# The first attention's output bias as one fp32r product of full height instead of four one-row fp32 products

## The reference

```python
y = jnp.moveaxis(ys, 0, 1).reshape(b, t, H) @ Wout.T + bout
z = x + y
mu = z.mean(-1, keepdims=True)
var = ((z - mu) ** 2).mean(-1, keepdims=True)
return (z - mu) / jnp.sqrt(var + LN_EPS) * ln_g + ln_b
```

## Time and profile before

| what | us |
|---|---|
| median of 3 runs (1953.53 to 1953.88) | 1953.6 |
| the profiled execution's own time | 1950.02 |
| its span, first to last instruction | 1948.2 |
| PE busy | 1700.6 (87%) |
| DVE busy | 1412.5 (73%) |
| ACT busy | 1026.3 (53%) |
| POOL busy | 572.8 (29%) |
| FFN's first product starts at | 385.40 |

### The profile page before, as it was taken

One profiled execution on the slowest core, in us unless ns is written; L12 is line 12 of the kernel. 1 busy time (PEld: TensorE's weight loads), 2 busy tenths in 40 slices (PEclk: granted clock), 3 DMA queues, 4 the chain that ended last, 5 costly groups with the idle time before them and its releaser, 6 DMA issues.

```text
span 1948.2 us, 26315 instructions
## 1 busy us (share of the span) xinstructions
PE 1700.6 (87%) x7480; PEld 1301.4 (67%) x7480; DVE 1412.5 (73%) x2367; ACT 1026.3 (53%) x1765; POOL 572.8 (29%) x441
## 2 busy tenths in 40 slices
PE   3677676599999999999688898999699999999998
PEld 2344344387787778787366666666487787778787
DVE  6899998667777777777367666665577777777776
ACT  1121111166666666655376766767566666666665
POOL 1455555501101110400167666767501101110100
PEclk8788777599999999999699989989899999999999
DMA  2000001100000000100000000000100000000001
GB/s 77 0 1 0 0 0 33 50 1 16 16 1 16 16 0 0 33 1 1 0 1 1 1 1 0 0 1 1 33 1 17 17 0 17 16 0 0 0 1 43
DMA packets 23716, 20.14 MB, mean 10 GB/s; under 512 B 1626, under 2 KB 19166, under 8 KB 23646
## 3 DMA queue, kind: packets, MB, share of 16 engines
q1 hardware_dynamic: 23646, 19.29, 3.3%
HBM read 17.18 MB, written 2.10 MB: 10 GB/s over the span
## 4 chain that ended last, share of the span: by engine, by line
PE 69%; DVE 10%; issue 9%; POOL 7%; ACT 3%; DMA 0%; SPq 0%; DVEq 0%; POOLq 0%; ACTq 0%
PE pair L347 12%; PE pair L349 12%; PE pair L348 12%; PE bank L347 7%; PE bank L348 6%; PE bank L349 6%; POOL ARENA_R L735 3%; DVE XN L390 2%; DVE ARENA_R L1348 2%; PE pair L1168 2%; POOL ARENA L646 1%; DVE ARENA L457 1%; PE pair L1097 1%; PE pair L1098 1%; DVE ARENA L1486 1%
## 5 line engine op out<-in xcount | busy, mean ns | idle before, releaser
L1344 DVE TENSOR_TENSOR ARENA<-ARENA,pair 128x512 f32<-128x512 f32 x512 | 351.5, 687 | 289.9 <-PE pair L349 212.8
L772 ACT ACTIVATE ARENA<-bank 128x512 f32<-128x512 f32 x512 | 304.2, 596 | 347.2 <-PE bank L349 345.8
L347 PE MATMUL pair<-ARENA_R 128*128 128x512 f32 (+1 forms) x1080 | 427.2, 396 | 32.4 <-DVE ARENA_R L1348 17.9
L348 PE MATMUL pair<-ARENA_R 128*128 128x512 f32 (+1 forms) x1080 | 421.9, 391 | 0.0
L349 PE MATMUL pair<-ARENA_R 128*128 128x512 f32 (+1 forms) x1080 | 421.9, 391 | 0.0
L1348 DVE TENSOR_TENSOR ARENA_R<-ARENA,ARENA_R 128x512 fp32r<-128x512 f32 x512 | 375.6, 735 | 11.9
L766 ACT ACTIVATE ARENA_R<-ARENA 128x512 fp32r<-128x512 f32 x512 | 321.2, 627 | 64.5 <-DVE ARENA L1344 64.0
L735 POOL TENSOR_TENSOR ARENA_R<-ARENA,ARENA_R 128x512 fp32r<-128x512 f32 x192 | 250.3, 1317 | 120.2 <-ACT ARENA L909 115.5
L347 PEld LDWEIGHTS pair<-ARENA_R 128*128 128x128 f32 x1080 | 203.8, 189 | 86.3 <-DVE ARENA_R L1348 23.0
L589 POOL CAST ARENA_R<-ARENA 128x1536 fp32r<-128x1536 f32 x12 | 23.2, 1937 | 756.4 <-PE pair L349 756.4
L349 PEld LDWEIGHTS pair<-ARENA_R 128*128 128x128 f32 x1080 | 203.6, 189 | 42.8
(11 more groups left out here) (207 smaller groups left out, 2463.8 us busy)
## 6 DMA issues: line engine op xcount, KB each, us to landing
ARENA<-in_L_ffn_Wg_dram SPq DMA_DIRECT2D x16, 256.0 KB, 2.7
ARENA<-in_L_ffn_Wu_dram SPq DMA_DIRECT2D x16, 256.0 KB, 3.1
ARENA<-in_L_ffn_Wd_dram SPq DMA_DIRECT2D x16, 256.0 KB, 3.6
X<-in_L_attn_a_x_dram SPq DMA_DIRECT2D x8, 256.0 KB, 6.5
out_dram<-X SPq DMA_DIRECT2D x8, 256.0 KB, 2.3
CST<-in_tables_dram SPq DMA_DIRECT2D x1, 832.5 KB, 4.7
ARENA<-in_tables_dram SPq DMA_DIRECT2D x1, 768.0 KB, 4.3
CST<-in_tables_dram SPq DMA_DIRECT2D x1, 259.0 KB, 4.9
```

Source lines behind the costliest of these rows:

```text
L347: pe.matmul(dst, wh, xh, start=start, stop=False)
L348: pe.matmul(dst, wh, xl, start=False, stop=False)
L772: act.activation(SG[:, k % 2, :], bank[k % 2], ACT.Silu).then_inc(s.sil, 1)
L1344: v.tensor_tensor(HF[:, k, :], SG[:, k % 2, :], bank[2 + k % 2], ALU.mult).then_inc(s.mul, 1)
```

## The change

The bias becomes a matrix of 128 rows, BBA, whose row 0 is the fp32r rounding of `bout`, row 1 the rest that the rounding left, and all others zero. One fp32r product of ONESR (all ones, 128x128) with BBA, repeated four times by a zero stride to 512 columns, writes the whole bank with the bias; the four products with WOUT then add to it.

```diff
                     pe.wait_ge(A.y, old.n + 1)
+                    pe.matmul(by_sub(bank[4]), ONESR[:, :], spread(BBA[:, :], SUB), start=True, stop=False,
+                              skip_group_check=True)
                     for k in range(SUB):
                         cols = slice(k * P, (k + 1) * P)
-                        pe.matmul(bank[4][:, cols], Y[:, old.p, cols], WOUT[:, :], start=True, stop=False)
-                        x = pe.matmul(bank[4][:, cols], ONES[0:1, :], BROW[:, 0:C], start=False, stop=True)
+                        x = pe.matmul(bank[4][:, cols], Y[:, old.p, cols], WOUT[:, :], start=False, stop=True,
+                                      skip_group_check=True)
                     x.then_inc(A.z, 1)
```

```diff
@@ SP
-            sp.dma_start(BROW[:, 0:C], row(a_bout)).then_inc(ld.ba, 16)
+            sp.wait_ge(pr.ones, 3)
+            sp.dma_start(BA0[0:2, :], row(a_bout).broadcast_to([2, C])).then_inc(ld.ba, 16)
@@ POOL
             g.memset(HALF[:, :], -0.5).then_inc(pr.ones, 1)
+            g.memset(BA0[:, :], 0.0).then_inc(pr.ones, 1)
+            g.wait_ge(pr.ones, 3)
+            g.tensor_copy(ONESR[:, :], ONES[:, :]).then_inc(pr.selr, 1)
...
             g.wait_ge(ld.ba, 80)
+            g.wait_ge(ld.tables_a, 16)
+            g.tensor_copy(BBH[:, 0:C], BA0[:, :]).then_inc(pr.bqkr, 1)
+            g.wait_ge(pr.bqkr, 1)
+            g.tensor_tensor(BA1[:, :], BA0[:, :], BBH[:, 0:C].bitcast(F32), ALU.subtract).then_inc(pr.bqkr, 1)
+            g.wait_ge(pr.bqkr, 2)
+            g.tensor_scalar(BA1[:, :], BA1[:, :], cst("pick")[:, 1:2], None, ALU.mult).then_inc(pr.bqkr, 1)
+            g.tensor_scalar(BA0[:, :], BBH[:, 0:C].bitcast(F32), cst("pick")[:, 0:1], None, ALU.mult).then_inc(pr.bqkr, 1)
+            g.wait_ge(pr.bqkr, 4)
+            g.tensor_tensor(BBA[:, :], BA0[:, :], BA1[:, :], ALU.add).then_inc(pr.bqkr, 1)
             run_steps(g, step)
...
-            g.tensor_copy(ONESR[:, :], ONES[:, :]).then_inc(pr.selr, 1)
@@ PE, ahead of its steps
-            pe.wait_ge(pr.ones, 2)
+            pe.wait_ge(pr.ones, 3)
+            pe.wait_ge(pr.bqkr, 5)
+            pe.wait_ge(pr.selr, 1)
```

More of the change, by code:

```diff
@@ L67, in constants @@
     c["sign"] = np.where((np.arange(P) // HA) % MA == 0, 1.0, -1.0)[:, None]
+    c["pick"] = np.eye(P, 2, dtype=np.float32)
     inv = (1.0 / 10000.0 ** (np.arange(0, DB, 2, dtype=np.float32) / DB)).astype(np.float32)
@@ L78, in constants @@
     c["kpat"] = kpat
-    c["pick"] = np.eye(P, 2, dtype=np.float32)
     for j in range(NJ):
@@ L193, in program @@
         WOB = sb("WOB", [P, C])
-        BROW = sb("BROW", [1, C])
+        BBA = sb("BBA", [P, C], F32R)
+        BA0 = sb("BA0", [P, C])
+        BA1 = sb("BA1", [P, C])
         GB = sb("GB", [P, 2, C])
@@ L554, in _ @@
             sp.dma_start(STAGED[:, :], consts[:, CS:]).then_inc(ld.tables_b, 16)
-            sp.wait_ge(pr.ones, 3)
+            sp.wait_ge(pr.ones, 4)
             sp.dma_start(BB[0:2, 0:C], row(b_bo).broadcast_to([2, C])).then_inc(ld.bb, 16)
@@ L1312, in _ @@
             pe.wait_ge(f[0].done, NT)
-            pe.wait_ge(pr.bqkr, 6)
+            pe.wait_ge(pr.bqkr, 11)
             for k in range(4):
@@ L1551, in step @@
                     norm_lo(v, n_a, nxt, bank[0], XH[:, nxt.p, :], XL[:, nxt.p, :])
-            v.wait_ge(pr.ones, 2)
+            v.wait_ge(pr.ones, 3)
             run_steps(v, step)
```

## The result

The changed kernel takes 1965.27 us, the median of 4 runs (1964.09 to 1966.64), against 1953.57 us of the kernel before (1953.49 to 1953.88): 1.006 times as long, with a 95% interval of 1.0042 to 1.0077. PE has less to do in it, and yet it is slower, by 11.7 us between the medians. The forecast was 1965. The profiled execution took 1965.29 us, 15.3 more than that of before; its first FFN starts at 398.35 instead of 385.40, so 12.95 us of it are in the first attention. The other 2.3 lie behind it, where the change takes one POOL cast away and adds nothing. Whole executions spread too: on one chip 35 of the kernel before ran from 1944.64 to 1958.25.

A forecast was written before the change was run, and what follows sets the result against it. The prediction took a first-attention step to be bound by DVE, with a hold by POOL. Prologue +2.7, clock +11.1 and tile 7 -2.45 gave +11.35 us on the median 1953.6: 1965, range 1953 to 1969.

The forecast's parts named there:

- PE per tile, 2.45 us less: Output projection: four bias products (2.88 us) go, one fp32r product (0.43) comes, 2.45 us less per tile.
- On the path only at tile 7: Tiles 0 to 6 gain nothing, as L390 ends behind POOL's L651; at tile 7 all 2.45 us come off.
- SP and the moved cast: nothing: Prologue: SP's wait for the third POOL memset and the ONESR cast moved into POOL's idle time cost nothing.
- Prologue, +2.7: Prologue: five POOL operations ahead of the first VE and RSTD delay DVE's first L390 by 2.7 us.
- The held case: Prologue: DVE's L1437 holds the new POOL subtraction until 16.33, putting VE and RSTD's end at 20.1 against 17.23, +2.9 us.
- The clock, 6 x 1.85 = 11.1: Tiles 2 to 7: PE idles before the transposes, loses full clock before L347, 1.85 us per step, 11.1 in all.
- the cheaper of two readings: Price per half-clock step read as 1.84 to 2.19 us; 1.85 taken, the clock returning within the projections.
- Rival A: PE reaches L347 at full clock as before; +0.3 us, 1953.9, no change; chance 0.13.
- B: L390 isn't held by L651, so 0.41 us comes off seven times; -4.2 us, 1949.4; chance 0.06.
- C: The clock falls and comes back only behind the denominators; +23 us, 1977; chance 0.03.
- D: The fp32r bias product takes 2.9 us, no faster than what it replaces; +2.7 us, 1956.3; chance 0.05.

The follow-up runs named there:

- nobias: The kernel before with the four one-row bias products of the output projection left out, nothing added: 1964.42 us, ratio 1.0049.
- grouped: The kernel before with the eight output projection products reordered, the four with WOUT first, then the four one-row ones: 1960.79 us, ratio 1.0046.
- hold: The changed kernel with PE's numerators of tiles 1 to 7 waiting for DVE's last scan of the tile: 1955.32 us, ratio 0.9997.
- the prologue alone: The changed kernel's prologue with the four one-row products of before in every step, the prepared rows unused: 1957.56 us, ratio 1.0014.
- fill12: The changed kernel with twelve unused 512-column products on PE between the numerators and the next tile's transposes: 1965.38 us, ratio 1.0051.
- fill20: The changed kernel with twenty unused 512-column products on PE between the numerators and the next tile's transposes: 1960.07 us, ratio 1.0040.
- best: The changed kernel with the numerators of tiles 1 to 7 held until the last scan and the bias row prepared earlier: 1951.51 us, ratio 0.9993.

## Why the prediction was right

Point by point, as it was put:

1. **PE per tile, 2.45 us less.** Mis-sized: 3.49 (5.78 to 2.29). The fp32r product's 0.43 was too little: L1113 begins 0.59 us behind it, as L348 does behind L347, the first of its row, on tile 0. But the four with WOUT, which I left at 0.72, take 0.43 each (170.30 to 172.00). I had charged the one-row products with half of the eight; nobias shows two thirds, 3.92, and grouped says why.
2. **On the path only at tile 7.** Right: DVE's wait of 0.41 went away, and L392's end stayed 0.87 behind L657's. The Trainium skill's page "SBUF — State Buffer", section "SBUF: two separate sides", has this as an exclusive lock of a shared port pair, and the trace agrees: L392 started sooner and ran 4.59 us instead of 4.07. At tile 7 the gain was 3.36 instead of 2.45, by the error of point 1.
3. **SP and the moved cast: nothing.** Right: the bias row is issued at 5.98, before the change at 5.97.
4. **Prologue, +2.7.** Right: 2.66, and by the course foreseen, the subtraction held by L1455 (1.87 against 0.48 us). The held case as worked out gave 2.9; 2.7 was the length of the five operations alone.
5. **The clock, 6 x 1.85 = 11.1.** The mechanism is shown by hold (idle time moved, cost gone) and nobias (work gone, cost there). The idle time before the transposes of tiles 2 to 7 was 3.8 to 5.5 us, where I had put 2 to 3: the output projection was shorter than forecast, and in the step shown the clock was back 2.1 us into the numerators, so that they took 4.63 us instead of 6.62. The size of the cost: five steps from tile 2 to 7 went from 196.97 to 208.39 us, 2.28 each, and tile 7 from its transposes to its output projection from 59.35 to 62.12, 2.77: together 14.2 instead of 11.1. I had taken the cheaper of two readings, with the clock back within the projections. In the step shown DVE's fourth rope product came 4.61 us after the first projection, but on tile 2 5.52 and on tile 7 5.48, for the clock came back later (at 187.8 in the step shown, 3.4 us behind the first projection; on tile 2 5.4, on tile 7 5.3). The way from tile 0's transposes to tile 2's became 0.55 us shorter, which I hadn't foreseen; the prologue alone made it 0.24 shorter.

The sum of the trace: 2.67 - 0.55 + 14.19 - 3.36 = 12.95 us to the FFN's start, where I had 11.35. Two terms were too small, one up and one down, and part of the error cancelled. The 1.6 us that remain don't show between the medians, which are 11.7 us apart; that is the spread between executions, and the lucky part.

Of the argument for point 5, one step doesn't hold in general: that a gap of 2 us costs the clock. It was right that the longer gap here would. But fill12, with 2.06 to 2.25 us, kept it through the transposes and lost it in the projections; fill20 lost it there with 0.55 and 1.48, best with 0.10 and 1.54; and the kernel before kept it with 0.62 and 1.48. What decides between these cases stays open. On the page "TensorE: Matmul & The Clock Gate" of the Trainium skill, section "Loop structure matters more than you think", waits between bursts put PE back to its slow clock; the trace agrees, with a wait shorter than the page's example. By that example alone, as the prediction worked it out, this term would have been zero; it was 14.2.

Rival A (the clock holds) is refuted by the stretches above and by the first projections of tiles 2 to 7, 0.59 and then 0.43 us apart on all six. B is refuted by L392's end, and D by L1109, from whose start to L1113 it is 0.59 us. C is refuted by its size (14.2 us, not 23) and by the clock's return before the denominators: latest on tile 6, where it was full by 273.2 and they begin at 273.30.

The 2.3 us by which the profiled executions differ behind the first attention need no cause in the change: nobias, with the code of before there, differs by 3.7.

## What to carry to other kernels

Where an engine other than PE bounds a stage, shorten PE's work only after asking what PE does in the time freed: idle time just ahead of dense products can cost their clock, here 14 us against 3.4 gained. Moving the idle time, by a wait ahead of work that nobody needs yet so that it ends right before the dense part, cost nothing measurable (0.9997) and kept the clock in five of six steps (best) or all six (hold), which filler products did in two of six at most. It is no guarantee: look at the clock in every step. Preparation that is done once belongs ahead of the wait on which its engine would idle anyway.

## What the runs showed of the hardware

- Eight fp32 products that alternate between 128-row and one-row weights took 5.78 us at half clock, the same eight in two groups 4.00; a one-row product by itself cost as much as a full-height one, 0.50.
- PE busy without a pause on the output projection (162.78 to 168.56 before the change) did not bring the clock back: it was at half up to 174.5, 5.9 us into the numerators behind it, and on the other tiles 2.9 to 5.6 us into them. After the change it came back 1.4 to 3.6 us into them.
- How late the clock comes back varies from step to step: in the changed kernel 2.9 to 6.1 us behind the first projection, and its steps were 41.2 to 42.3 us long. In fill12 and grouped the clock fell later, in the projections, and the steps were 40.9 to 41.1.
- The clock fell in the projections behind gaps of 0.55 and 1.48 us (fill20) and 0.10 and 1.54 (best), and held behind 0.62 and 1.48 (before).
- Executions of the unchanged kernel spread from 1944.64 to 1958.25 us (35 on one chip), from 1948.28 to 1957.67 (19 on another) and from 1953.49 to 1953.88 (4 on the one of the result).
